# First stages with stores by 32 rows, stationary router weights, Bm in both row halves; denominators once per eight heads

## What is computed

```python
# 1 memory attention
xB = jnp.einsum('bsd,de->sbe', x, Bm)
h_final = scan(h = h @ A + xB[s])                       # over 256 tokens
h_proj = h_final @ W_imp.T
importance = softmax(einsum('bsd,bd->bs', x, h_proj))
token_pref = softmax(einsum('bsd,nd->bsn', x, W_router))   # 64 neurons
neuron_w = einsum('bs,bsn->bn', importance, token_pref); neuron_w /= neuron_w.sum(-1)
shared_compress = einsum('bn,ndr->bdr', neuron_w, compress)
Q = einsum('bsd,bdr->bsr', x, shared_compress)
scores = einsum('bsr,nr->bsn', Q, K) / sqrt(128)        # 8192 keys, top 8, softmax, sum of V rows
# 2 cross attention: 16 heads of 64 over a context of 256 rows
attn = softmax(clip(mask(q k^T / 8), -5, 5)); out = (attn @ v) @ Wo + bo
# 3 expert feed-forward with hard routing (controller, f1, relu, f2)
```

## Time and profile before

| | |
|---|---|
| median of three runs | 1467.55 us (1467.44 to 1468.25) |
| the profiled execution's own time | 1467.52 us |
| its span, first to last instruction | 1465.7 us |
| PE / PEld / DVE / ACT / POOL busy | 91% / 68% / 74% / 49% / 50% |
| mean granted TensorE clock | 0.966 |

### The profile page before, as it was taken

One profiled execution on the slowest core, in us unless ns is written; L12 is line 12 of the kernel. 1 busy time (PEld: TensorE's weight loads), 2 busy tenths in 40 slices (PEclk: granted clock), 3 DMA queues, 4 the chain that ended last, 5 costly groups with the idle time before them and its releaser, 6 DMA issues.

```text
span 1465.7 us, 25223 instructions
## 1 busy us (share of the span) xinstructions
PE 1337.5 (91%) x9837; PEld 1002.9 (68%) x9837; DVE 1081.4 (74%) x1625; ACT 716.0 (49%) x1357; POOL 730.0 (50%) x1010
## 2 busy tenths in 40 slices
PE   8936688999999999999999999999999989568998
PEld 5714475868686877777776868686867757347765
DVE  2218989888888888888888888888888861037567
ACT  0215346464655555555546464555555532225455
POOL 0325326564747465655656574747475653530224
PEclk9878889999999999999999999999999999879999
DMA  9323111222213131212121222222131211162324
GB/s 365 137 103 103 57 40 51 73 65 63 70 55 85 50 85 51 70 51 69 51 69 52 72 68 67 66 57 81 48 81 38 72 37 38 30 202 83 118 63 127
DMA packets 62902, 115.84 MB, mean 79 GB/s; under 512 B 9728, under 2 KB 43456, under 8 KB 61632
## 3 DMA queue, kind: packets, MB, share of 16 engines
q1 hardware_dynamic: 45600, 66.62, 14.8%
q0 software_dynamic: 14848, 41.96, 9.8%
q10 hardware_dynamic: 2336, 5.66, 1.0%
HBM read 103.45 MB, written 10.75 MB: 78 GB/s over the span
## 4 chain that ended last, share of the span: by engine, by line
PE 75%; DVE 16%; DMA 2%; issue 2%; POOL 1%; ACT 1%; SPq 1%; another core or an unknown queue 1%; POOLq 0%; DVEq 0%; ACTq 0%
PE proj_bank L360 35%; PE score_bank L360 28%; PE sim_bank L360 8%; DVE cand_val L1006 5%; DVE cand_idx L1007 4%; DVE x_sum L1030 3%; PE score_bank L673 2%; DMA shared_compress<-xT_by_step 1%; PE sim_bank L673 1%; DVE dispatchedT L1144 1%; DVE den_recip L1054 1%; PE sim_bank L607 1%; POOL exp L1234 1%; POOL v_rows L1205 0%
## 5 line engine op out<-in xcount | busy, mean ns | idle before, releaser
L772 ACT COPY score_row<-score_bank 128x512 f32<-128x512 f32 x512 | 299.7, 590 | 189.4 <-PE score_bank L360 109.4
L1006 DVE MAX8 cand_val<-score_row 128x8 f32<-128x2048 f32 x128 | 292.3, 2283 | 92.0 <-ACT score_row L772 68.7
L1205 POOL DMA_INDIRECT v_rows<-in_V,top_idx x256 | 249.0, 973 | 188.1 <-DVE top_idx L1020 105.9
L1234 POOL TENSOR_SCALAR exp<-exp,exp_bound 128x256 f32<-128x256 f32 x512 | 247.5, 501 | 142.1 <-ACT exp L784 141.3
L1007 DVE FIND_INDEX8 cand_idx<-cand_val,score_row 128x8 uint32<-128x2048 f32 x128 | 292.5, 2285 | 0.0
L360 PE MATMUL score_bank<-keysT_hi,qT_hi 128*128 128x512 f32 x512 | 218.3, 426 | 30.0 <-ACT score_row L772 26.3
L360 PE MATMUL score_bank<-keysT_hi,qT_lo 128*128 128x512 f32 x512 | 204.9, 400 | 0.0
L360 PE MATMUL score_bank<-keysT_lo,qT_hi 128*128 128x512 f32 x512 | 204.6, 400 | 0.0
L784 ACT ACTIVATE exp<-sim_bank 128x512 f32<-128x512 f32 x256 | 139.3, 597 | 111.4 <-PE sim_bank L360 107.5
L360 PE MATMUL sim_bank<-qT_heads,kT 64*128 64x256 f32 x1024 | 146.9, 406 | 8.4 <-ACT exp L784 8.4
L360 PEld LDWEIGHTS score_bank<-keysT_hi,qT_hi 128*128 128x128 f32 x512 | 98.0, 191 | 68.4 <-ACT score_row L772 30.2
(11 more groups left out here) (171 smaller groups left out, 2237.4 us busy)
## 6 DMA issues: line engine op xcount, KB each, us to landing
kT<-den_scratch SPq DMA_DIRECT2D x64, 256.0 KB
x_pair<-x_scratch SPq DMA_DIRECT2D x32, 256.0 KB, 2.8
f_quads<-in_f POOLq DMA_DIRECT2D x32, 256.0 KB, 5.3
comp_then_wqkv_raw<-in_comp SPq DMA_DIRECT2D x6, 1024.0 KB, 18.5
xT_by_step<-in_xTs SPq DMA_DIRECT2D x4, 1024.0 KB, 9.4
keysT_raw<-in_KmT ACTq DMA_DIRECT2D x8, 512.0 KB, 8.2
xT_in<-in_xT SPq DMA_DIRECT2D x16, 256.0 KB
x_sum<-in_x SPq DMA_DIRECT2D x32, 128.0 KB, 2.1
```

The source lines that it names most:

```text
L772: nc.scalar.copy(srow[n // PER % 2][:, i * CB:(i + 1) * CB], scb[n % 3]).then_inc(sem("score_evac"), 1)
L1006: own(nc.vector.max(cv[:, tile, cs], srow[g % 2][:, :]))
L1205: pool.indirect_dma_start(out=vg[:, k, :], out_offset=None, in_=V_rows, in_offset=bass.IndirectOffsetOnAxis(ap=i8[:, tile, k:k + 1], axis=0))\
L1234: last = nc.gpsimd.tensor_scalar(ex[i % NEX][:, k, :], ex[i % NEX][:, k, :], ub[:, k, c:c + 1], E_LO, ALU.min, ALU.max)
```

## The change

- **Stores.** Eight stores as before, but two times four: after four groups, and after eight, one store for each 32 partitions of `scs`, with 32 as the outermost size on both sides and 8 KB from each partition.
- **Router.** The weights (64 columns) are stationary and the tokens are streamed, 512 columns at a time: four products per router, the even batches into the upper and the odd ones into the lower 64 rows of the PSUM bank. The logits now lie transposed, so ACT copies them to `router_T` (`router_out`), and PE transposes them back (`router_transpose`), four transposes per router. DVE's work on them moves later, and `router(3)` and two sums now stand between the importance maximum and the weights' diagonal. The exponential of router 3 stands behind the importance exponential on ACT, and the first key casts move between the routers' copies.
- **Bm.** A, its powers and Bm^T lie in both halves of the partitions; `bm_powers(hf)` does two products on different rows into two banks, and is called twice. Four copies by ACT as before.
- **Warming products.** `warm(n)`: n products of 128 x 128 x 128 with zeros, whose result nothing reads; six as soon as `h_proj_diag` is zeroed, and six more between the first powers.
- **Denominators.** The products leave `values`; `denominators(c, h)` does sixteen for eight heads in one go, after `values(c, 1)` and after `values(c, 3)`. `exp` has ten buffers, and ACT waits for the denominators eight heads at a time.
- **Memory.** `den_recip` now shares its place with `x1T_lo`, so `x1_lo` waits for the stores of the reciprocals. `compress` block 7 is loaded into the place of `wo`, so Wo is loaded later, by SP behind the weights, and the output products wait for it.

```diff
-NEX = 6
+NEX = 10
...
-            for g in range(NG_SC):
-                sp.wait_ge(sem(("sc_act", "sc_dve")[g % 2]), g // 2 + 1)
-                sp.dma_start(scd_st[g], scs[:, g * 512:(g + 1) * 512]).then_inc(sem("sc_stored"), 16)
+            for half in range(2):
+                sp.wait_ge(sem("sc_act"), 2 * half + 2)
+                sp.wait_ge(sem("sc_dve"), 2 * half + 2)
+                for c in range(4):
+                    sp.dma_start(scd_st[half, c], scs[32 * c:32 * c + 32, half * CH:(half + 1) * CH])\
+                        .then_inc(sem("sc_stored"), 16)
...
+            def warm(n):
+                for _ in range(n):
+                    mm(pp[0][:, 0:P], hm[:, 0, 0:4, :].rearrange("p b m -> p (b m)"),
+                       hm[:, 1, 0:4, :].rearrange("p b m -> p (b m)"))
...
+            def bm_powers(hf):
+                for k in range(KT):
+                    r = slice(k * SD, (k + 1) * SD)
+                    last = mm((sp_, pp)[hf][k][:, :], bmt[r, :], pw[r, 8 * hf:8 * hf + 8, :].rearrange("p a b -> p (a b)"))
+                last.then_inc(sem("ba_pe"), 1)
...
-                for b in range(8):
-                    for k in range(KT):
-                        last = mm(rt_bank[n][:, b * NC:(b + 1) * NC], xs[:, k, h, b0 + b, :],
-                                  wrt[:, k, :], start=(k == 0), stop=(k == KT - 1))
+                for k in range(KT):
+                    for o in range(2):
+                        last = mm(rt_bank[n][o * NC:(o + 1) * NC, :], wrt[:, k, :], xs[:, k, h, b0 + o:b0 + 8:2, :],
+                                  start=(k == 0), stop=(k == KT - 1))
...
+            def router_transpose(n):
+                pe.wait_ge(sem("router_evac"), n + 1)
+                for i in range(4):
+                    last = nc.tensor.transpose(tr_bank[n][:, i * P:(i + 1) * P], rtT[:, n, i * P:(i + 1) * P], idn[:, :])
+                last.then_inc(sem("routerT_pe"), 1)
...
-                if j % 2 == 0:
-                    need(pe, "rden_done", 2 * c + j // 2)
-                for k in range(KT):
-                    for q in range(4):
-                        last = mm(den[32 * q:32 * q + 32, :], sel[:, j % 2, :], ex[(H * c + 4 * j + q) % NEX][:, k, :],
-                                  start=(j % 2 == 0 and k == 0), stop=(j % 2 == 1 and k == KT - 1))
+            def denominators(c, h):
+                need(pe, "rden_done", 2 * c + h)
+                for j in range(2):
+                    for k in range(KT):
+                        for q in range(4):
+                            last = mm(den[32 * q:32 * q + 32, :], sel[:, j, :],
+                                      ex[(H * c + 8 * h + 4 * j + q) % NEX][:, k, :],
+                                      start=(j == 0 and k == 0), stop=(j == 1 and k == KT - 1))
                 last.then_inc(sem("den_full"), 1)
...
                         values(c, j - 1)
+                        if j == 2:
+                            denominators(c, 0)
...
-                    need(act, "den_full", (i - NEX) // 4 + 1)
+                    need(act, "den_full", (i - NEX) // 8 + 1)
...
+                need(dve, "rden_stored", 16 * 2 * batch)
```

More of the change, by code:

```diff
@@ L155, in build @@
         nd = sb(pre, "neuron_diag", [P, B, KT])
-        cst = [sb(pre, f"comp_stage_{i}", [P, CH]) for i in range(2)]
+        cst = sb(pre, "comp_stage", [P, CH])
         scs = xs[:, 0, :, :, :].rearrange("p h b s -> p (h b s)")
@@ L188, in build @@
         x1 = [sb(work, f"x1_{i}", [P, TT, D]) for i in range(2)]
-        x1h, x1l = sb(work, "x1T_hi", [P, KT, S], F32R), sb(work, "x1T_lo", [P, KT, S], F32R)
+        x1h = sb(work, "x1T_hi", [P, KT, S], F32R)
+        shared = work.enter_context(ExitStack())
+        rden = sb(shared, "den_recip", [P, S])
+        shared.close()
+        x1l = sb(work, "x1T_lo", [P, KT, S], F32R)
         ct = sb(work, "ctxT_in", [P, KT, S])
@@ L195, in build @@
         ex = [sb(work, f"exp{i}", [P, KT, S]) for i in range(NEX)]
-        rden = sb(work, "den_recip", [P, S])
         main.close()
@@ L373, in power @@
                 m = 7 if r == 7 else n
-                rows = SD if r < 3 else P
-                last = mm(scp[r % 2][0:rows, 0:m * SD], tpw[r][:, 0:rows],
+                last = mm(scp[r % 2][:, 0:m * SD], tpw[r][:, :],
                           src[0:SD, 1:1 + m, :].rearrange("p a b -> p (a b)"))
@@ L555, in _ @@
                         key = ("WO", p, tile)
+                        need(pe, "wo_in", 16)
                         need(pe, "ot_done", 2 * (p + 1))
@@ L583, in _ @@
                     values(c, NP // 2 - 1)
+                    denominators(c, 1)
                 if mid:
@@ L745, in _ @@
                 .then_inc(sem("imp_exp"), 1)
-            for n in range(4, NK // KW):
+            router_exp(3)
+            for n in range(2, NK // KW):
                 key_hi(n)
@@ L930, in router, with router_sum @@
                                         ALU.subtract).then_inc(sem("router_sub"), 1)
-            for r in range(7):
+            def router_sum(n):
+                dve.wait_ge(sem("router_exp"), n + 1)
+                nc.vector.tensor_reduce(rsm[:, 8 * n:8 * n + 8], rte[:, 8 * n:8 * n + 8, :], AX, ALU.add)\
+                    .then_inc(sem("router_sum"), 1)
+            for r in range(8):
                 power(r)
-            router(0)
-            power(7)
-            router(1)
             dve.wait_ge(sem("pre_pe"), PRE_PE["scan1"])
@@ L945, in _ @@
                 last = nc.vector.tensor_copy(hm[:, k, :, :].rearrange("p (c j) m -> p c (j m)", j=4)[:, :, 0:4 * 32:33],
-                                             sp_[0][:, 32 + k * B:32 + (k + 1) * B].rearrange("p (c j) -> p c j", j=4))
+                                             pp[1][:, 32 + k * B:32 + (k + 1) * B].rearrange("p (c j) -> p c j", j=4))
             last.then_inc(sem("pre_dve"), 1)
-            router(3)
-            for n in range(4):
-                dve.wait_ge(sem("router_exp"), n + 1)
-                nc.vector.tensor_reduce(rsm[:, 8 * n:8 * n + 8], rte[:, 8 * n:8 * n + 8, :], AX, ALU.add)\
-                    .then_inc(sem("router_sum"), 1)
-            dve.wait_ge(sem("router_sum"), 4)
-            after("router_rec", nc.vector.reciprocal(rrc[:, :], rsm[:, :]), 1)
+            router(1)
+            router(2)
+            router_sum(0)
+            router_sum(1)
             dve.wait_ge(sem("pre_pe"), PRE_PE["imp_pe"])
@@ L957, in _ @@
                 .then_inc(sem("pre_dve"), 1)
+            router(3)
             dve.wait_ge(sem("imp_exp"), 1)
@@ L960, in _ @@
             nc.vector.tensor_scalar(impe[:, :], impe[:, :], imx[:, 2:3], None, ALU.mult).then_inc(sem("pre_dve"), 1)
+            router_sum(2)
+            router_sum(3)
+            dve.wait_ge(sem("router_sum"), 4)
+            after("router_rec", nc.vector.reciprocal(rrc[:, :], rsm[:, :]), 1)
             dve.wait_ge(sem("pre_pe"), PRE_PE["impT_pe"])
@@ L1051, in den_inverse @@
                 n = 2 * c + h
-                need(dve, "den_full", 2 * n + 2)
+                need(dve, "den_full", n + 1)
                 need(dve, "rden_stored", 16 * n)
```

107 lines of the change are left out of this document (57 added, 50 removed).

## The result

| | before | after |
|---|---|---|
| median, us (runs) | 1467.62 (1467.44 to 1468.25, 4) | 1434.32 (1433.56 to 1435.45, 4) |
| profiled execution, us | 1467.52 | 1435.45 |
| its span, us | 1465.7 | 1433.4 |

The changed kernel takes 0.9773 of the time before (95% interval 0.9756 to 0.979): 33.3 us less. The forecast was 1427.5, 6.8 us too low; the result lies in the range (1416 to 1442) and in the likeliest case's own (1419 to 1436).

What follows compares the result with a forecast made beforehand. TensorE carries 75% of the chain, so a gain must shorten its sequence or start it earlier. Terms -16.5 - 8.8 + 2.0 + 1.5 - 12 - 6.1 = -39.9 from 1467.52 gave 1427.5 us, range 1416 to 1442.

Steps and rivals of the forecast that it cites:

- Part 1: PE up to the end of the first scan step: warming products, Bm pairs, routers 0 and 1, earlier clock rise; -16.5 us.
- The bound beside it: PE up to the first scan step's end: if the clock rises only in router group 0, the gain is -12.8 us.
- Rival 3: The clock is up from the first powers, giving 4.5 us more at the start: 1421.5 us; 13%.
- Part 2: From the first scan step to the end of the importance products: shorter routers, clock holding; -8.8 us.
- Part 3: From importance to compress products: added DVE work +2.0 us, compress products partly at the lower clock +1.5.
- The DVE term: Between importance and compress products, a router and two sums now stand ahead on DVE: +2.0 us.
- The clock term: First compress products may run at the lower clock after PE's 4.5 us gap: +1.5 us, bounds 0 and +4.
- Part 4: Stores of the compressed matrix land sooner after the last copy, at half the loads' rate, some 210 GB/s: -12 us.
- Part 5: The batch turns: 0.28 us less per turn times 15, and 1.9 in the first turn; -6.1 us.
- Rival 4: Half the front's gain is eaten by something released by time and not by the stores: 1447 us; 2%.
- Rival 5: Slower: x1T_lo waits for the second reciprocal's store and PE waits at its Q products; about 1475 at 25 us; 3%.
- Rival 2: Stores stay slow because 2 KB pieces of DRAM, not the number of engines, set 99 GB/s: 1438.5 us; 10%.

Runs made afterwards that it cites:

- c: The changed kernel with all warming products left out: 1434.22 us.
- d: The changed kernel with 28 more warming products (10, 10 and 8) in PE's three waits between importance and compress products: 1433.18 us.
- g: The changed kernel with eight stores of 128 rows by 512 columns as before, but the destination's outermost dimension 32 (a measurement, not usable): 1434.07 us.
- h: The changed kernel without warming at the start, with 17 warming products before the compress products, Wo loaded later, 22 warming products in the feed-forward stage: 1430.83 us.
- a: The changed kernel with the eight stores of before (128 rows by 512 columns, destination's outermost dimension 4): 1445.20 us.
- i: The changed kernel with its 32-row stores in four quarters, 16 stores of 128 KB, issued by SP and ACT: 1441.43 us, as the unaltered one beside it.
- b: The kernel before with the turns' change alone (denominators per eight heads, ten exp buffers, shared den_recip, Wo behind the weights): 1463.57 us, ratio 0.9987.
- e: The changed kernel with Wo's load moved on SP behind the loads for batch 1's shared projection: 1434.81 us.

## Why the prediction was right, and where it was off

**Part 1** (-16.5; measured -14.0). The Bm pairs were right (2.01 each), though the fourth of the old products took 1.71 and not 2.0, which is 0.3. The step that failed is "the upper level from about 20 us, in the second Bm pair": it came behind router group 0, which took 3.61 us instead of 1.8. That is the term mis-sized, by 1.8, with 0.3 in the eighth power (1.18).

The bound beside it does not come out of its own terms: with router group 0 at the lower level they give -14.7 and not -12.8. Of the reason given, PE's early work, the warming products are no part: without them the rise comes no later (*c*). The +1.0 for them was right by luck. They cost nothing in the changed kernel, and the first Bm pair is 1.05 us later than the first Bm product was (15.18 against 14.13) because the powers are now made in both halves: the first three take 1.28, 1.42 and 1.85 us in *c*, and took 0.91, 1.13 and 1.55. In *d* and *g*, with the same code up to there, this part ends at 37.3 and 36.9 us instead of 35.26, so its gain varies by 2 us between executions. Rival 3, a clock that is up from the first powers, came true for the powers alone. What brings the lasting rise from within the scan step to 25 us, Bm in pairs or routers of 512 columns, no run separates.

**Part 2** (-8.8; measured -9.0). Right: the routers take 1.72 and 1.82, the clock held.

**Part 3** (+3.5; measured +4.5). The DVE term was right: from the importance products to the neuron-weight products 4.42 us instead of 2.56, so +1.9 against +2.0. The clock term had the right mechanism at the wrong products. I charged 1.5 to the compress products; the products directly behind the wait paid 2.65 (6.41 instead of 3.76), and by the time the compress products began the clock was back (7.12, unchanged). *d* and *h* show the cause.

**Part 4** (-12; measured -11.8, and 11.9 in *a*). Right, and the cause with it: *g* against *a* changes the order alone. The busy share went from 26% to 95% and the rate from 99 to between 232 and 281 GB/s, short of the loads' 429. 128 rows per store (*g*), or two blocks of rows at once (*i*), landed 4.0 and 2.6 us sooner; both have smaller last pieces, but the engine time of a 2 KB piece (88 and 101 ns instead of 117) shows that the number of rows is a limit of its own. The landing came 7.0 us after the last copy where the sum had 6.6, but in other pieces: the rate was 261 and not 210 GB/s, while the sum let 2.1 MB flow evenly from 82.1 us. The last store was issued 2.85 us after the last copy (0.67, 1.10 and 0.89 us for the three ahead of it) and landed 4.17 us later. By the rule that the Trainium skill gives in DMA: Bandwidth & Descriptors (why a DMA increments its semaphore by 16), an outermost size of 4 keeps a DMA on 4 engines; *a* (26% busy) against *g* (87%) agrees. By what the Trainium skill gives in SBUF — State Buffer (port swizzle), 32 rows reach half the ports, with 189 GB/s for one transfer of 1 MiB; the 117 ns agree in direction, and the 261 GB/s of four queued stores from four blocks of rows are above it.

**Part 5** (-6.1; measured -8.4). Per turn -0.27 against -0.28, the group 1.93 against 1.86. In the first turn, `den_recip` to `den_recip` fell from 10.96 to 8.78, -2.2 against -1.9. This part differs between the sets: from the first `den_recip` to the first output product it is 27.2 us before and 25.0 in the changed kernel and in *a* to *d*, but 25.8 to 27.8 in the eight profiles of the other two sets, which have no profile of the kernel before beside them. "The last turn" at 0 was wrong: the last three periods, which lack part of the score work, took 67.67, 57.57 and 49.15 instead of 68.09, 59.39 and 49.40, -2.5 in all, and *b* has the same (67.67, 57.56, 49.25). Two turns of before at 69.0 and not 68.8 make the rest. So only 12 periods, and not 15, show the 0.27.

**What the sum left out.** "It carries through because the weight loads, first scores and the DVE-bound start are all released by the stores' landing" failed in two places. Wo's load, costed at nothing, stands in SP's queue ahead of the second `sc_in`, which now landed at 89.7: 3.0 us, shown by *b* and *e*, though the moved load was worth only 0.5 at the end of the start-up. And the prediction treated everything behind the front as shifted without change. The feed-forward stage took 5.3 us more: 3.2 behind two waits of PE in which the clock now fell, 0.9 from a later rise at its start, 1.3 unexplained. That the shift of 37 us brought the falls about isn't shown (*c* lies at nearly the same place and has only the second of them). Rival 4 had put a loss behind the front, but of half its gain and by something released by time; what was lost is 7 us, in other ways. The account closes: the five parts as measured make -38.7; of the early loss of 3.0, 1.3 is regained by the first `den_recip`; the stage adds 5.3, and last output group to logits gives 0.7: -38.7 + 1.7 + 5.3 - 0.7 = -32.4, the span's -32.3. That the forecast is only 6.8 us off owes something to luck: parts 1 and 3 gave 3.5 less than forecast and part 5 2.3 more.

Rival 5 (x1T_lo waiting for the reciprocals' store) did not occur: no wait of that kind stands in the turns. (By its own figures 25 us would have given 1473 and not 1475.) Rival 2 is excluded by *g*, where the pieces of DRAM are the same 2 KB and hold an engine as long as before (88 and 86 ns).

## What to carry to other kernels

Look at the outermost dimension of both sides of a DMA: with 4 on one side a quarter of the engines worked, with 32 on both sides the share was 91 to 95%. Let each store read many partitions too (128 rows here held an engine 88 ns per 2 KB piece, 32 rows 117). Check with the busy share and the rate together, since one limit can be cured while the other still holds. A wait of PE of 1.2 to 1.5 us on the critical path cost the products behind it half the clock in some profiles and nothing in others, so price a restructuring at the products behind the new waits, and let a range take in that a stage nobody touched took from 160.8 to 166.2 us. When a load changes queues, list what now stands behind it, however late its own data is wanted.

## What the runs showed of the hardware that I had not expected

- A clock that is raised ahead of the first work can be lost before that work needs it: in the changed kernel it was up in the first powers and down again by 10 us, and the lasting rise came no earlier than without the warming products (*c*).
- Chips differ by more than most of these edits: the same kernel 1434.3 and 1441.4 us. On the slower one six turns take 0.3 to 1.0 us more at a granted clock of 1.00; the cause stays open.
- Warming products of 128 columns have a price of their own, 0.22 us each even at the upper level (*d*): ten in a wait of 1.4 us cost a good part of what they save.
